# A graph network kernel: four groups of a row norm done by PE and ACT beside the sort, eight more loaded beside it

## The chip, the cores and the metric

One core of one Trainium2 chip. The metric is the device time of one execution in microseconds (us). PE is the matrix engine (TensorE), DVE the vector engine, ACT the scalar engine, POOL is GpSimd, SP only issues transfers.

## The reference, cut to what matters

There are 50,000 nodes with 256 features each and 12,500 edges, sorted by destination.

```python
x = _layernorm(x + gat(x, edges))      # attention over edges, relu(out + bias)
x = _layernorm(x + conv(x, src, dst))  # three max-convolutions with batch norm
def _layernorm(x, axis=-1, eps=1e-05):
    m = jnp.mean(x, axis=axis, keepdims=True)
    v = jnp.var(x, axis=axis, keepdims=True)
    return (x - m) / jnp.sqrt(v + eps)
```

A node that is the destination of no edge gets `relu(bias)` from the attention. So the kernel norms `x + relu(bias)` for all nodes ("the norm of all nodes"), and later overwrites the rows of the nodes that edges lead to.

## The kernel before

**Stages.** (1) The sort: 12,800 keys lie in a tile of 128 x 256 elements; DVE makes a bitonic sort of them (`sort_dve`, line 400 and on). Exchanges inside a partition (lines 426, 427) need only DVE. For k from 8 to 14, exchanges across partitions go by way of PE: DVE flips signs (line 418), PE transposes two blocks of 128 x 128 (line 500, `sort_pe`), DVE exchanges the transposed keys (lines 437 to 441), and the same again back. That is 14 turns, numbered 0 to 13 here; each waits for the one before. (2) `lists_dve` (lines 513 to 535) decodes the keys to lists of indices. (3) The edge stage, 25 tiles of 512 edges: POOL gathers rows of x (line 682, eight gathers a tile), PE turns them (line 696) and multiplies (lines 706, 712), ACT copies between (line 723) and writes h to the large buffer `big` (line 728), DVE copies the scores (line 735), SP stores the destination rows to `x_dst` (line 739) and the scores (line 743). (4) The softmax over edges on DVE (lines 751 to 841). (5) The message stage (from line 873), then three convolutions, the last state, and a dense pass over all rows (lines 1290 to 1343).

**The norm of all nodes** runs beside stages 3 and 4, in 40 groups (0 to 39): 39 of 1280 rows, ten rows to a partition, 1.31 MB each, and a rest of 80 rows. A ring `pre` of four buffers holds them. For group g, ACT's queue issues the load (`pre_load`, line 608). DVE adds relu(bias) to the whole group (line 625), takes statistics of ten rows (line 628) and joins them (line 634) (`pre_stats`). ACT takes the root (line 643, `pre_std`). DVE makes factor and shift with a Newton step in six small instructions (lines 652 to 660, `pre_finish`). ACT norms ten rows (line 668, `pre_norm`) and issues the store (`pre_store`, line 614). The four first loads are issued by ACT at the start, which then has nothing to do until the first edge tile is turned.

**The order of the work** is written by hand, one program for each engine at the end of the function. On DVE, edge tile t is followed by the finish of group t - 1 and the statistics of group t; so 25 groups (`EARLY = NS = 25`) go with the edge tiles, five stand between the steps of the softmax, and ten after it (the tail), before the message stage. On ACT, `pre_turnover(g)` (norm, store, load of the group three further on) stands once in each step of the edge stage. SP issues the setup loads, then waits for the lists. POOL builds constants, gathers for the edge stage, scatters the table of slots (lines 595, 588), and waits for all stores of the norm before its first scatter of message rows (line 964).

PE uses PSUM banks 5 and 6 in the sort and bank 7 for small things; 0 to 4 are unused there. `big` is written first by the edge stage.

Of the kernel before, what the change touches and what calls it, by code (L numbers as in the profile page):

```python
# [50 lines left out]
PRE_RING = 4  # L51
assert 0 < PTAIL <= P
# [5 lines left out]
def gnn(nc, x, src, dst, w, att_src, att_dst, bias, theta_t, phi_t, gammas, betas, out):  # L58
    ctx = ExitStack()
    with ctx:  # L60
# [77 lines left out]
        s_pre_x = [sem(f"pre_x_{b}") for b in range(PRE_RING)]  # L138
        s_pre_sum = sem("pre_sum")
# [107 lines left out]
        pre = part_of(8192, PRE_RING * PR * D).rearrange("p (b r f) -> p b r f", b=PRE_RING, r=PR)  # L247
        stat = sb("stat", [P, 2, PR, 6])
# [56 lines left out]
        def in_steps(stages, count):  # L305

            for s in range(count + max(lag for lag, _ in stages)):
                for lag, f in stages:
                    if 0 <= s - lag < count:
                        f(s - lag)  # L310

# [88 lines left out]
        def sort_dve(v):  # L400
# [30 lines left out]

            def exchange_turned(source, bit):
                nonlocal n, cur
                a = source.rearrange("p (x t b) -> p x t b", t=2, b=1 << bit)
                c = sort_buf[cur].rearrange("p (x t b) -> p x t b", t=2, b=1 << bit)
                o = sort_buf[1 - cur].rearrange("p (x t b) -> p x t b", t=2, b=1 << bit)
                v.tensor_copy(c[:, :, 1, :], a[:, :, 1, :]).then_inc(s_sort, 1)
                n += 1
                done()
                v.tensor_tensor(o[:, :, 0, :], a[:, :, 0, :], c[:, :, 1, :], ALU.min).then_inc(s_sort, 1)  # L440
                v.tensor_tensor(o[:, :, 1, :], a[:, :, 0, :], c[:, :, 1, :], ALU.max).then_inc(s_sort, 1)
                n += 2
                cur = 1 - cur
                done()
# [47 lines left out]
        def sort_pe(pe):  # L492
# [4 lines left out]
            for i, (n, cur) in enumerate(SORT_MARKS):  # L497
                pe.wait_ge(s_sort, n)
# [104 lines left out]
        def pre_load(a, g):  # L603
            rows, p, r = node_rows(g)
            b, u = g % PRE_RING, g // PRE_RING
# [3 lines left out]

        def pre_store(a, g):  # L610
            rows, p, r = node_rows(g)
            b = g % PRE_RING
            a.wait_ge(s_pre_normed, g + 1)
            a.dma_start(x1_dram[rows, :].rearrange("(p r) f -> p r f", r=r), pre[0:p, b, 0:r, :]).then_inc(s_pre_stored[b], 16)

        def rbias_dve(v):
            v.wait_ge(s_bias, 16)
            v.tensor_scalar(rbias_ps, rbias[:, :], 0.0, None, ALU.max).then_inc(s_rbias, 1)
            v.wait_ge(s_rbias, 1)

        def pre_stats(v, g):
            rows, p, r = node_rows(g)
            b, u, e = g % PRE_RING, g // PRE_RING, g % 2
            v.wait_ge(s_pre_x[b], 16 * (u + 1))
            v.tensor_tensor(pre[0:p, b, 0:r, :], pre[0:p, b, 0:r, :], rbias_ps[0:p, :].unsqueeze(1).to_broadcast([p, r, D]), ALU.add).then_inc(s_pre_sum, 1)  # L625
            v.wait_ge(s_pre_sum, g + 1)
            for n in range(r):
                m = v.bn_stats(stat[0:p, e, n, :], pre[0:p, b, n, :])  # L628
            m.then_inc(s_pre_stat, 1)
            v.wait_ge(s_pre_stat, g + 1)  # L630
# [6 lines left out]
        def pre_std(a, g):  # L637
            rows, p, r = node_rows(g)
            e = g % 2
            a.wait_ge(s_pre_mv, g + 1)  # L640
            if g > 1:
                a.wait_ge(s_pre_newton, 4 * (g - 1))
            a.activation(std[0:p, e, 0:r], mv[0:p, e, 0:r, 1], ACT.Sqrt, bias=eps_b[0:p, :]).then_inc(s_pre_std, 1)

        def pre_finish(v, g):
# [7 lines left out]
            v.wait_ge(s_pre_newton, 4 * g + 1)  # L653
            v.scalar_tensor_tensor(d, mv[0:p, e, 0:r, 1], EPS, near, ALU.add, ALU.mult).then_inc(s_pre_newton, 1)
            v.scalar_tensor_tensor(off, mv[0:p, e, 0:r, 0], -1.0, near, ALU.mult, ALU.mult).then_inc(s_pre_newton, 1)
            v.wait_ge(s_pre_newton, 4 * g + 2)
            v.scalar_tensor_tensor(d, d, -0.5, near, ALU.mult, ALU.mult).then_inc(s_pre_newton, 1)
            v.wait_ge(s_pre_newton, 4 * g + 4)
# [3 lines left out]
        def pre_norm(a, g):  # L662
# [3 lines left out]
            for n in range(r):  # L666
                o = pre[0:p, b, n, :]
# [57 lines left out]
        def gat_keep_h(a, t):  # L725
            for j in range(2):
# [139 lines left out]
        def msg_dve(v):  # L866
            v.wait_ge(s_h_kept, 2 * NS)

            def sums(t):
# [9 lines left out]
                else:  # L879
                    v.wait_ge(s_pre_stored[0], 16 * len(range(0, PG + 1, PRE_RING)))  # L880
# [77 lines left out]
        def x1_pool(pl):  # L958
            for b in range(PRE_RING):
                pl.wait_ge(s_pre_stored[b], 16 * len(range(b, PG + 1, PRE_RING)))  # L960
# [42 lines left out]
        def conv_sync(sp, l):  # L1003
            def masks(t):
                if l == 0 and t == 0:
                    for k in range(PRE_RING):
                        sp.wait_ge(s_pre_stored[k], 16 * len(range(k, PG + 1, PRE_RING)))
# [372 lines left out]
        def _(act):  # L1380
            act.wait_ge(s_ids, 32)
            for g in range(PRE_RING):
                pre_load(act, g)
            act.wait_ge(s_const, CONST)
            act.wait_ge(s_params, PARAMS)

            def pre_turnover(g):
                pre_norm(act, g)
                pre_store(act, g)
                if 1 <= g and g - 1 + PRE_RING <= PG:  # L1390
                    pre_load(act, g - 1 + PRE_RING)
            for s in range(NS + 2):
                if s < NS:
                    gat_keep(act, s)
                if 1 <= s <= NS:
                    gat_keep_h(act, s - 1)
                    pre_std(act, s - 1)
                if 2 <= s:
                    pre_turnover(s - 2)
# [100 lines left out]
```

## Time and profile before

| what | us |
|---|---|
| median of 3 runs (2014.74 to 2016.46) | 2015.37 |
| the profiled execution, its own time | 2019.85 |
| its span, from first to last instruction | 2018.1 |
| PE busy | 1183.2 |
| DVE busy | 1293.8 |
| ACT busy | 909.1 |
| POOL busy | 976.3 |
| transfers, 436.12 MB | 216 GB/s mean |

The span is what the rows below are numbered by, from 0. The difference of 1.75 us between the span and the execution's own time lies around it. Busy times overlap: engines run beside each other, and only where one waits for another does a time reach the end. A busy share over the whole span is a mean over stages that have different limits; the rows below are taken stage by stage. In a row of the timeline, the bracket at the end is the idle time of that engine just before, and what ended it. For a float32 product PE shows two records.

### The profile page before, as it was taken

The numbers are of one execution on the slowest core, as the hardware profiler recorded it, in microseconds if no ns is written. First come the engines' busy times: TensorE is split into PE (matmuls) and PEld (weight loads), VectorE is DVE, ScalarE is ACT, GpSimd is POOL, SyncE is SP. The second block draws the span as 40 slices with busy tenths as digits, with TensorE's granted clock in tenths as the row PEclk, the third lists the DMA queues.
The fourth block names the chain that finished last, engine by engine and source line by source line (L and its number), as shares of the span: only waits on it lengthen the run. The fifth ranks groups of instructions, "written<-read, shape, count | busy, mean of one in ns | idle before, by whom it ended". The sixth has DMA issues, their size and how long they took to land. (4 is left out here: it accounts for less than half of the span.)

```text
span 2018.1 us, 16817 instructions
## 1 busy us (share of the span) xinstructions
PE 1183.2 (59%) x3962; PEld 635.5 (31%) x3962; DVE 1293.8 (64%) x3151; ACT 909.1 (45%) x2286; POOL 976.3 (48%) x1033
## 2 busy tenths in 40 slices
PE   1177878730027773699995899969999675000000
PEld 0033333310003331355552455534544564000000
DVE  7746666689879995245553456635666432778887
ACT  0047657664542222244442356634554321556555
POOL 1176565677606777777772764325451577000000
PEclk9999889865555555799997899989999888555555
DMA  3069889987954553588884588747663454898998
GB/s 123 20 187 341 327 315 345 319 252 210 345 195 126 158 165 109 159 255 262 262 258 120 112 175 198 183 126 126 134 140 79 150 182 158 316 356 339 353 349 316
DMA packets 177486, 436.12 MB, mean 216 GB/s; under 512 B 28900, under 2 KB 108906, under 8 KB 157420
## 3 DMA queue, kind: packets, MB, share of 16 engines
q1 hardware_dynamic: 107964, 219.04, 32.0%
q0 software_dynamic: 44800, 100.49, 20.1%
q10 hardware_dynamic: 24624, 115.51, 16.4%
q8 instruction: 33, 0.54, 0.1%
q14 instruction: 65, 0.53, 0.1%
HBM read 257.16 MB, written 182.32 MB: 218 GB/s over the span
## 5 line engine op out<-in xcount | busy, mean ns | idle before, releaser
L1157 DVE TENSOR_TENSOR_SCAN arena<-arena,ps 128x512 f32<-128x512 f32 x150 | 191.3, 1277 | 267.3 <-PE ps L1082 254.3
L1052 POOL DMA_INDIRECT arena<-agg,slot x200 | 189.0, 945 | 206.8 <-PE ps L1072 112.3
L682 POOL DMA_INDIRECT arena<-x,idx x200 | 189.2, 946 | 192.6 <-DVE idx L535 85.5
L1082 PE MATMUL ps<-arena 128*128 128x512 f32 x600 | 276.0, 604 | 0.0
L1092 PE MATMUL ps<-arena 128*128 128x512 f32 x600 | 269.7, 592 | 0.0
L1338 ACT ACTIVATE arena<-arena 128x256 f32<-128x256 f32 x391 | 156.6, 402 | 145.9 <-DVE arena L1307 145.9
L1034 POOL DMA_INDIRECT arena<-x,idx x200 | 189.2, 946 | 62.0 <-issue 59.1
L668 ACT ACTIVATE arena<-arena,shift,inv 128x256 f32<-128x256 f32 x391 | 196.2, 589 | 38.5 <-DVE shift L660 38.5
L927 PE MATMUL ps<-arena,head_of 8*128 8x512 f32 x100 | 93.7, 1088 | 159.1 <-DVE arena L882 119.8
L1161 DVE TENSOR_TENSOR ps<-arena,ps 128x512 f32<-128x512 f32 x150 | 104.1, 696 | 110.4 <-PE ps L1092 110.4
L1072 PE MATMUL ps<-ident,arena 128*128 128x128 f32 x800 | 114.0, 289 | 103.6 <-DMA arena<-agg,slot 50.0
L1128 ACT ACTIVATE arena<-ps,bn_shift,bn_scale 128x512 f32<-128x512 f32 x100 | 72.8, 774 | 215.7 <-PE ps L1072 215.5
L1092 PEld LDWEIGHTS ps<-arena 128*128 128x128 f32 x600 | 114.0, 190 | 143.5 <-issue 142.5
L1307 DVE TENSOR_TENSOR arena<-arena 128x2560 f32<-128x2560 f32 (+1 forms) x40 | 110.6, 2765 | 58.9 <-DMA arena<-x 58.7
L1082 PEld LDWEIGHTS ps<-arena 128*128 128x128 f32 x600 | 110.8, 195 | 111.9 <-issue 101.1
L964 POOL DMA_INDIRECT x<-big,idx x100 | 99.7, 997 | 87.4 <-ACT big L954 56.7
L1276 POOL DMA_INDIRECT x<-arena,idx x100 | 99.4, 994 | 84.8 <-DVE arena L1267 56.0
L1072 PEld LDWEIGHTS ps<-ident,arena 128*128 128x128 f32 x800 | 94.4, 147 | 129.0 <-DMA arena<-agg,slot 52.9
L628 DVE BATCH_NORM_STATS2 stat<-arena 128x6 f32<-128x256 f32 x391 | 131.6, 411 | 1.4
L1120 ACT ACTIVATE arena<-ps 128x512 f32<-128x512 f32 x100 | 55.2, 595 | 170.4 <-PE ps L1072 169.9
L588 POOL DMA_INDIRECT slot<-slot_of,idx x100 | 96.2, 962 | 71.4 <-SPq L1020 35.3
L625 DVE TENSOR_TENSOR arena<-arena,ps 128x2560 f32<-128x2560 f32 (+1 forms) x40 | 110.2, 2755 | 17.6 <-DMA arena<-x 17.6
(183 smaller groups left out, 2155.6 us busy)
## 6 DMA issues: line engine op xcount, KB each, us to landing
arena<-x ACTq DMA_DIRECT2D x39, 1280.0 KB, 10.7
x<-arena ACTq DMA_DIRECT2D x39, 1280.0 KB, 6.5
arena<-x SPq DMA_DIRECT2D x39, 1280.0 KB, 8.2
out<-arena SPq DMA_DIRECT2D x39, 1280.0 KB, 5.4
agg<-arena SPq DMA_DIRECT2D x50, 512.0 KB, 4.7
arena<-not_same SPq DMA_DIRECT2D x75, 256.0 KB, 3.9
arena<-last_of SPq DMA_DIRECT2D x75, 256.0 KB, 5.1
x_dst<-arena SPq DMA_DIRECT2D x25, 512.0 KB, 6.5
```

Source lines behind the costliest of these rows:

```text
L625: v.tensor_tensor(pre[0:p, b, 0:r, :], pre[0:p, b, 0:r, :], rbias_ps[0:p, :].unsqueeze(1).to_broadcast([p, r, D]), ALU.add).then_inc(s_pre ...
L628: m = v.bn_stats(stat[0:p, e, n, :], pre[0:p, b, n, :])
L668: m = a.activation(o, o, ACT.Identity, scale=inv[0:p, b, n:n + 1], bias=shift[0:p, b, n:n + 1])
L682: pl.indirect_dma_start(rows_in[:, par, a, g, :], None, x[:, :], bass.IndirectOffsetOnAxis(ap=idx[:, k, t * G + g:t * G + g + 1], axis=0)) ...
L1034: pl.indirect_dma_start(conv_in[:, b, a, g, :], None, x1_dram[:, :], bass.IndirectOffsetOnAxis(ap=idx[:, k, t * G + g:t * G + g + 1], axis ...
L1052: pl.indirect_dma_start(conv_in[:, b, 1, g, :], None, agg_dram[l - 1][:, :], bass.IndirectOffsetOnAxis(ap=slot[:, t * G + g:t * G + g + 1] ...
L1072: m = pe.transpose(turn_bank[j][:, g * P:(g + 1) * P], conv_in[:, b, a, g, j * P:(j + 1) * P], ident[:, :])
L1082: m = pe.matmul(far_bank[j], thp[:, l, 0, k, j * P:(j + 1) * P], far_t[:, par, k, :], start=(k == 0), stop=(k == 1))
L1092: m = pe.matmul(near_bank[j], thp[:, l, 1, k, j * P:(j + 1) * P], near_t[:, par, k, :], start=(k == 0), stop=(k == 1))
L1157: v.tensor_tensor_scan(runmax[:, par, j, :], mask[:, par, :], far_bank[j], initial, ALU.add, ALU.max).then_inc(s_conv_scan, 1)
L1307: v.tensor_tensor(y, y, c_rows[0:p, :].unsqueeze(1).to_broadcast([p, r, D]), ALU.add).then_inc(s_dense_y, 1)
L1338: m = a.activation(unused[0:p, n, :], y_tile[0:p, b, n, :], ACT.Square, scale=1.0 / ROOT, accum_out=msq[0:p, b, n:n + 1])
```

## The change

Groups 0 to 3 are no longer done by DVE. PE adds the bias: for each of a group's ten rows it multiplies the row tile by the identity and adds the product of a row of ones and relu(bias), into banks 0 to 4 (`rows_pe`). ACT copies the sum back to the ring and sums each row (`rows_sum_act`), makes the negative mean, squares the centred row with a sum (`rows_square_act`), takes the root, and norms as before. DVE keeps the six small instructions (`rows_finish`), three times placed just before it waits for a turn of the sort (turns 1, 5 and 10), the fourth time after the sort. PE does groups 0 and 1 before turn 0, group 2 before turn 2 and group 3 before turn 6. DVE takes relu(bias) before the sort (`row_bias_dve`); after it, a copy goes to PSUM.

Groups 4 to 11 are loaded at the start by SP (`big_load_sync`, after the setup) into the last 80% of `big`, each with its own semaphore, and are normed and stored from there beside edge tiles 0 to 7. ACT waits for the store of such a group before it writes h over it. The ring holds groups 0 to 3 and 12 to 39; its loads follow in that order. The edge stage still has 25 groups beside it, now 4 to 28; five stand in the softmax (29 to 33) and six after it (34 to 39).

```diff
@@ -49,6 +49,8 @@
 PRE_RING = 4
+PRE_SORT = 4
+PRE_BIG = 8
...
@@ -308,6 +320,40 @@
+        def in_big(g):
+            return PRE_SORT <= g < PRE_SORT + PRE_BIG
...
+        RING_USES = PG + 1 - PRE_BIG
...
+        def pre_rows(g):
+            if in_big(g):
+                lo = NS * 2 * SUP - (PRE_SORT + PRE_BIG - g) * PR * D
+                return big[:, lo:lo + PR * D].rearrange("p (r f) -> p r f", r=PR)
+            return pre[:, ring_use(g) % PRE_RING, :, :]
...
@@ -429,6 +475,11 @@
+            def beside_turn():
+                for g, at in enumerate((1, 5, 10)):
+                    if turns == at:
+                        rows_finish(v, g)
...
@@ -457,11 +508,13 @@
             for k in range(8, 15):
                 flip_partition(k - 7)
+                beside_turn()
                 turns += 1
                 v.wait_ge(s_sort_turned, 2 * turns)
...
+                beside_turn()
                 turns += 1
                 v.wait_ge(s_sort_turned, 2 * turns)
...
@@ -495,6 +548,9 @@
             for i, (n, cur) in enumerate(SORT_MARKS):
+                for g, at in enumerate((0, 0, 2, 6)):
+                    if i == at:
+                        rows_pe(pe, g)
                 pe.wait_ge(s_sort, n)
...
@@ -600,34 +656,102 @@
+        def big_load_sync(sp):
+            for k in range(PRE_BIG):
+                rows, p, r = node_rows(PRE_SORT + k)
+                sp.dma_start(pre_rows(PRE_SORT + k), x[rows, :].rearrange("(p r) f -> p r f", r=r)).then_inc(s_big_x[k], 16)
...
+        def row_bias_dve(v):
+            v.wait_ge(s_bias, 16)
+            v.tensor_scalar(rbias[:, :], rbias[:, :], 0.0, None, ALU.max).then_inc(s_rbias, 1)
+
+        def rows_pe(pe, g):
+            if g == 0:
+                pe.wait_ge(s_const, 8)
+                pe.wait_ge(s_rbias, 1)
+            loaded(pe, g)
+            for i in range(PR // 2):
+                if g:
+                    pe.wait_ge(s_row_ready, PR * (g - 1) + 2 * i + 2)
+                for n in range(2 * i, 2 * i + 2):
+                    o = bank[i][:, (n % 2) * D:(n % 2 + 1) * D]
+                    pe.matmul(o, ident[:, :], pre_rows(g)[:, n, :], start=True, stop=False)
+                    m = pe.matmul(o, ones[0:1, :], rbias[0:1, :], start=False, stop=True)
+                m.then_inc(s_row_sum, 1)
+
+        def rows_sum_act(a, g):
+            if g > 1:
+                a.wait_ge(s_row_squares, g - 1)
+            for n in range(PR):
+                a.wait_ge(s_row_sum, PR // 2 * g + n // 2 + 1)
+                a.activation(pre_rows(g)[:, n, :], bank[n // 2][:, (n % 2) * D:(n % 2 + 1) * D], ACT.Identity,
+                             accum_out=row_sum[:, n:n + 1]).then_inc(s_row_ready, 1)
+            a.wait_ge(s_row_ready, PR * (g + 1))
+            a.activation(row_mean[:, g, :], row_sum[:, :], ACT.Copy, scale=-1.0 / D).then_inc(s_row_mean, 1)
+
+        def rows_square_act(a, g):
+            a.wait_ge(s_row_mean, g + 1)
+            for n in range(PR):
+                m = a.activation(row_unused[:, n, :], pre_rows(g)[:, n, :], ACT.Square, bias=row_mean[:, g, n:n + 1],
+                                 accum_out=row_var[:, g, n:n + 1])
...
+            a.activation(std[:, g % 2, :], row_var[:, g, :], ACT.Sqrt, scale=1.0 / D, bias=eps_b[:, :]).then_inc(s_pre_std, 1)
...
@@ -723,6 +846,10 @@
         def gat_keep_h(a, t):
+            for k in range(PRE_BIG):
+                lo = NS * 2 * SUP - (PRE_BIG - k) * PR * D
+                if lo < (t + 1) * 2 * SUP and t * 2 * SUP < lo + PR * D:
+                    a.wait_ge(s_big_stored[k], 16)
...
@@ -1344,11 +1469,12 @@
-        EARLY = NS
+        EARLY = PRE_SORT + NS
...
             setup_sync(sp)
+            big_load_sync(sp)
             lists_sync(sp)
...
             def pre_turnover(g):
                 pre_norm(act, g)
                 pre_store(act, g)
-                if 1 <= g and g - 1 + PRE_RING <= PG:
-                    pre_load(act, g - 1 + PRE_RING)
+                if not in_big(g) and ring_use(g) and ring_use(g) - 1 + PRE_RING < RING_USES:
+                    pre_load(act, ring_use(g) - 1 + PRE_RING)
+            rows_sum_act(act, 0)
+            rows_square_act(act, 0)
+            for g in range(1, PRE_SORT):
+                rows_sum_act(act, g)
+                pre_turnover(g - 1)
+                rows_square_act(act, g)
+            pre_turnover(PRE_SORT - 1)
+            act.wait_ge(s_params, PARAMS)
...
             keys_dve(dve)
+            row_bias_dve(dve)
             sort_dve(dve)
+            rows_finish(dve, PRE_SORT - 1)
             lists_dve(dve)
...
             for t in range(NS):
                 gat_score(dve, t)
                 if t:
-                    pre_finish(dve, t - 1)
-                pre_stats(dve, t)
+                    pre_finish(dve, PRE_SORT + t - 1)
+                pre_stats(dve, PRE_SORT + t)
```

## Rows read from the trace of the kernel before

**Rows 1.** The windows view by stage: window, its length, busy us (instructions) by engine, clock, DMA.

```profile
0.00:27.50 27.50, 0.98 (x8) 0.92 (x8) 22.25 (x75) 0.00 (x0) 7.31 (x33) 1.00 0.62 226
27.50:86.40 58.90, 9.64 (x28) 4.04 (x28) 44.16 (x174) 0.00 (x0) 0.00 (x0) 1.00 0.00 0
...
421.00:500.00 79.00, 3.01 (x13) 1.10 (x12) 75.34 (x190) 39.66 (x79) 62.17 (x56) 0.53 0.81 239
500.00:589.40 89.40, 3.75 (x4) 1.16 (x4) 72.82 (x256) 53.74 (x111) 39.57 (x41) 0.50 0.84 298
```

**Rows 2.** The timeline at the start of the message stage: start, us, engine, line.

```profile
589.38 1.22 DVE L873 TENSOR_TENSOR ps<-ps,big 128x1024 f32<-128x1024 f32 x1
...
614.64 1.02 POOL L964 DMA_INDIRECT x<-big,idx  x1 [56.69 <-ACT big L954]
```

**Rows 3.** The timeline of PE's turns in the sort.

```profile
27.51 0.69 PE L500 MATMUL ps<-ident,arena 128*128 128x128 f32 x2 [22.81 <-DVE arena L418]
...
34.41 0.69 PE L500 MATMUL ps<-ident,arena 128*128 128x128 f32 x2 [4.54 <-DVE arena L418]
...
49.78 0.69 PE L500 MATMUL ps<-ident,arena 128*128 128x128 f32 x2 [4.54 <-DVE arena L418]
```

**Rows 4.** The timeline of DVE where the sort ends and the decoding of the lists begins.

```profile
86.47 0.29 DVE L513 TENSOR_SCALAR arena<-arena 128x256 int32<-128x256 int32 x1
```

**Rows 5.** The first three loads of x, line 608: issue, and issue to landing.

```profile
L608 ACTq DMA_DIRECT2D arena<-x x3: 390/450/1119, 3.6 to 4.5; - x3
...
DMA to landing us min/median/max: 8.5/11.2/13.9
```

**Rows 6.** PE on 128x256 float32 products of line 1250, warm and after a gap.

```profile
1626.80 3.72 PE L1250 MATMUL ps<-center,arena 128*128 128x256 f32 x16 [2.09 <-DVE arena L1259]
...
1692.22 10.10 PE L1250 MATMUL ps<-center,arena 128*128 128x256 f32 x32 [3.28 <-DVE arena L1259]
```

**Rows 7.** Groups and timeline of ACT: a square with sum of one row, ten rows normed.

```profile
L1338 ACT ACTIVATE arena<-arena 128x256 f32<-128x256 f32 x390 | 156.2, 402 | 145.9 <-DVE arena L1307 145.9
...
419.02 5.01 ACT L668 ACTIVATE arena<-arena,shift,inv 128x256 f32<-128x256 f32 x10
```

**Rows 8.** DVE's finish of one group of the norm, first and last instruction.

```profile
458.38 0.21 DVE L652 RECIPROCAL ps<-std 128x10 f32<-128x10 f32 x1
...
459.11 0.16 DVE L660 SCALAR_TENSOR_TENSOR shift<-step,ps 128x10 f32<-128x10 f32 x1
```

**Rows 9.** DVE's copies of the scores, line 735, of tiles 1, 3, 4 and 24.

```profile
132.72 0.68 DVE L735 COPY score<-ps 8x512 f32<-8x512 f32 x1 [1.22 <-PE ps L706]
...
154.80 0.68 DVE L735 COPY score<-ps 8x512 f32<-8x512 f32 x1 [4.74 <-PE ps L706]
163.71 0.68 DVE L735 COPY score<-ps 8x512 f32<-8x512 f32 x1 [0.48 <-PE ps L706]
...
418.69 0.65 DVE L735 COPY score<-ps 8x512 f32<-8x512 f32 x1
```

**Rows 10.** Windows of the edge stage, and the waits that end on transfers.

```profile
93.80:163.70 69.90, 49.36 (x169) 23.60 (x169) 35.87 (x115) 29.32 (x55) 53.12 (x56) 0.93 0.63 197
163.70:421.00 257.30, 204.09 (x632) 90.06 (x632) 168.53 (x568) 171.05 (x345) 159.63 (x169) 0.89 0.92 324
...
POOL arena L682 <- DMA x_dst<-arena: 45.6, 17, 7.8
...
DVE arena L625 <- DMA arena<-x: 17.6, 11, 4.5
```

**Rows 11.** The timeline of DVE, additions of the bias (line 625) in the tail.

```profile
522.53 2.82 DVE L625 TENSOR_TENSOR arena<-arena,ps 128x2560 f32<-128x2560 f32 x1 [3.37 <-DMA arena<-x]
...
556.32 2.81 DVE L625 TENSOR_TENSOR arena<-arena,ps 128x2560 f32<-128x2560 f32 x1
...
564.53 2.81 DVE L625 TENSOR_TENSOR arena<-arena,ps 128x2560 f32<-128x2560 f32 x1
```

More of the change, by code:

```diff
@@ L138, in gnn @@
         s_pre_x = [sem(f"pre_x_{b}") for b in range(PRE_RING)]
+        s_big_x = [sem(f"big_x_{k}") for k in range(PRE_BIG)]
+        s_big_stored = [sem(f"big_stored_{k}") for k in range(PRE_BIG)]
+        s_row_sum = sem("row_sum")
+        s_row_ready = sem("row_ready")
+        s_row_mean = sem("row_mean")
+        s_row_squares = sem("row_squares")
         s_pre_sum = sem("pre_sum")
@@ L310, in in_steps, with ring_use, group_at, loaded @@
                         f(s - lag)
+        def in_big(g):
+            return PRE_SORT <= g < PRE_SORT + PRE_BIG
+        def ring_use(g):
+            return g if g < PRE_SORT else g - PRE_BIG
+        def group_at(use):
+            return use if use < PRE_SORT else use + PRE_BIG
+        RING_USES = PG + 1 - PRE_BIG
[4 more added lines that the diff above has]
+            return pre[:, ring_use(g) % PRE_RING, :, :]
+        def loaded(e, g):
+            if in_big(g):
+                e.wait_ge(s_big_x[g - PRE_SORT], 16)
+            else:
+                e.wait_ge(s_pre_x[ring_use(g) % PRE_RING], 16 * (ring_use(g) // PRE_RING + 1))
+        def all_stored(e):
+            for b in range(PRE_RING):
+                e.wait_ge(s_pre_stored[b], 16 * len(range(b, RING_USES, PRE_RING)))
+            for k in range(PRE_BIG):
+                e.wait_ge(s_big_stored[k], 16)
         def node_rows(g):
@@ L613, in pre_store @@
             a.wait_ge(s_pre_normed, g + 1)
-            a.dma_start(x1_dram[rows, :].rearrange("(p r) f -> p r f", r=r), pre[0:p, b, 0:r, :]).then_inc(s_pre_stored[b], 16)
+            a.dma_start(x1_dram[rows, :].rearrange("(p r) f -> p r f", r=r), pre_rows(g)[0:p, 0:r, :]).then_inc(stored, 16)
+        def row_bias_dve(v):
[14 more added lines that the diff above has]
+                m.then_inc(s_row_sum, 1)
@@ L666, in pre_norm @@
             for n in range(r):
[L667 removed]
+                o = pre_rows(g)[0:p, n, :]
                 m = a.activation(o, o, ACT.Identity, scale=inv[0:p, b, n:n + 1], bias=shift[0:p, b, n:n + 1])
@@ L725, in gat_keep_h @@
         def gat_keep_h(a, t):
+            for k in range(PRE_BIG):
+                lo = NS * 2 * SUP - (PRE_BIG - k) * PR * D
+                if lo < (t + 1) * 2 * SUP and t * 2 * SUP < lo + PR * D:
+                    a.wait_ge(s_big_stored[k], 16)
             for j in range(2):
@@ L879, in sums @@
                 else:
-                    v.wait_ge(s_pre_stored[0], 16 * len(range(0, PG + 1, PRE_RING)))
+                    v.wait_ge(s_pre_stored[0], 16 * len(range(0, RING_USES, PRE_RING)))
                 for j in range(2):
@@ L958, in x1_pool @@
         def x1_pool(pl):
-            for b in range(PRE_RING):
-                pl.wait_ge(s_pre_stored[b], 16 * len(range(b, PG + 1, PRE_RING)))
+            all_stored(pl)
             for t in range(NS):
@@ L1005, in masks @@
                 if l == 0 and t == 0:
-                    for k in range(PRE_RING):
-                        sp.wait_ge(s_pre_stored[k], 16 * len(range(k, PG + 1, PRE_RING)))
+                    all_stored(sp)
                 if l or t > 1:
@@ L1381, in _ @@
             act.wait_ge(s_ids, 32)
-            for g in range(PRE_RING):
-                pre_load(act, g)
+            for use in range(PRE_SORT):
+                pre_load(act, use)
             act.wait_ge(s_const, CONST)
-            act.wait_ge(s_params, PARAMS)
             def pre_turnover(g):
```

62 lines of the change are left out of this document (44 added, 18 removed).

## The prediction

> **What bounds the kernel now.** I read the windows by stage first, then the waits, then the timelines of the stages that the change touches. To 27.5 us DVE sorts inside each partition. From there to 86.4 it sorts across partitions: DVE is busy for 44.16 of 58.90 us, PE for 9.64, ACT not at all, and no byte moves [rows 1]. The sort is a chain between DVE and PE: DVE flips, PE transposes two blocks (0.69 us), DVE goes on. Between turn 1 and turn 2, and between turn 5 and turn 6, PE is idle for 4.54 us [rows 3]. The decoding starts at 86.47 [rows 4]. So three resources lie idle beside a chain that is itself critical: whatever is put on PE there is free only in so far as it fits between two turns.
>
> The edge stage follows, 25 tiles beside 25 groups of the norm. While few node groups move, two tiles take 22.08 us (copy of the scores of tile 1 at 132.72, of tile 3 at 154.80), 11.04 a tile; from tile 4 at 163.71 to tile 24 at 418.69 it is 254.98/20 = 12.75 a tile [rows 9]. In between the transfers went from 197 to 324 GB/s and from 0.63 to 0.92 of the engines; POOL waits 45.6 us in all for the stores of the destination rows, DVE 17.6 us for loads of x [rows 10]. The first pace is a loop over engines (score, statistics, root, norm, copy, product); the rest, 1.71 us a tile, is contention of transfers.
>
> The softmax and the tail follow. DVE is busy for 75.34 of 79 us to 500, and 72.82 of 89.4 us until the message stage starts [rows 1]; it is the bound, with 15 groups of the norm on it. In the tail one group follows the other by 564.53 - 556.32 = 8.21 us, and one stall for a load stands beside the first loads of the message stage [rows 11]. The message stage starts at 589.38, and POOL has by then been idle for long: its first scatter at 614.64 comes after 56.69 us of waiting [rows 2]. All later work starts from there, so what reaches 589.38 reaches the end.
>
> **Part 1, PE ahead of turn 0: +5.9 us.** PE does groups 0 and 1 before it looks at the first turn, each 10 products with the identity and 10 with the row of ones, on 256 columns of float32. A row of the same shape gives 16 records, two for each product, in 3.72 us [rows 6], so 0.2325 us a record; 20 products are 40 records, 9.3 us. After 3.28 us idle 32 records took 10.10 us, 2.7 us more than twice 3.72 [rows 6]: so I price a start from rest at 12.0 us. The first load is issued at 3.6 us and lands 8.5 us later, at 12.1; the second is there by 15.2 (issued near 4, 11.2 us) [rows 5]. Group 0 runs 12.1 to 24.1, group 1 to 33.4. Turn 0 stood at 27.51 [rows 3], so the sort waits 5.9 us. The relu of the bias ahead of the sort vanishes in this wait. SP's eight new loads are issued from 8.7 us on, behind the setup; no wait of SP stands behind them before the lists at 91 us, and their 10.5 MB have 60 us of idle transfer engines, so they cost nothing of their own. If they hold up group 0, the bound is the landing of the second load now, 3.1 us later. The Trainium skill ("DMA: Bandwidth & Descriptors", Queues, rings and completion order) says that each transfer engine serves the queues that have work in turn, packet by packet; by it ACT's first load would share from 8.7 us, and I estimate 1.4 us more for the sum. No row here has two such large queues at once in the setup.
>
> **Part 2, PE between the turns: +4.8 and +7.5 us.** Group 2 stands between turn 1 and turn 2: 9.3 us in a hole of 4.54 us, 4.8 us too many; PE has been busy just before, so I take the warm price. Group 3 stands before turn 6 after some 10 us in which PE only makes short turns with idle stretches as long as 4.54 us; I take the start from rest: 12.0 - 4.54 = 7.5 us. Below, both are warm and group 0 too: 3.2 + 4.8 + 4.8 us. Above, the engine stays at the lower of its two levels, 1.2 GHz, all through: 18.6 us a group, which gives 21.8 + 14.1 + 14.1 us for the three places.
>
> **Part 3, DVE: +1.5 us.** A finish takes 0.89 us (458.38 to 459.27) [rows 8]. Three of the four stand where DVE waits for a turn of 0.69 us anyway, 0.2 us each too many; the fourth, 0.9 us, comes after the sort and before the decoding, on the path. DVE waits in them for ACT's root. ACT has per group ten sums and ten squares, 0.402 us each, and ten norms, 5.01 us [rows 7]: 13 us, 52 for all four groups in a sort that then lasts until 105 us. Root 1 is ready some 10 us before turn 5, root 3 some 9 us before the sort ends; I charge nothing. If that cover were gone, each missing us would stand in the sort. Group 3 is normed and stored beside the decoding and the first gathers; ACT was not needed there before. Its wait for the parameters, now behind this, ends long before. Sort in all: 5.9 + 4.8 + 7.5 + 1.5 = +19.7 us, with bounds 13.7 and 51.4.
>
> **Part 4, the edge stage: -11 us.** It still norms 25 groups, so the loop of 11.04 us stays. But groups 4 to 11 lie in the buffer of h and their turnovers load nothing; groups 12 to 14 are loaded by the turnovers of groups 1 to 3. So for eight tiles 1.31 of some 4.2 MB a tile are gone (gathers 1.05, destination rows 0.52, load and store of a group 1.31 each). At 1.71 us a tile that is 13.7 us if all contention goes. The stores stay, so I take 11. Bounds: 0 (the stores alone are enough), and 20 (the ring also runs ahead afterwards, so that DVE's 17.6 us of waits shrink too). The new waits of ACT for the stores of groups 4 to 11 before it writes h start with tile 5; by then group 4 has been stored for three tiles. Nothing.
>
> **Part 5, the tail: -32.8 us.** Four groups fewer stand behind the softmax: 4 x 8.21 = 32.8 us, all DVE. ACT's norms, four loads and four stores go with them. Next after DVE would be POOL, which has 56.69 us of slack [rows 2]; the stage starts some 24 us earlier, so it holds. Bounds 28 (the stall at the first message loads grows) and 36.
>
> **Sum.** The profiled execution took 2019.85 us (span 2018.1). 2019.85 + 19.7 - 11 - 32.8 = 1995.8. The runs' median 2015.37 lies 4.5 us below the profiled one, so the forecast is **1991.3 us**. What follows the message stage is unchanged.
>
> **Rivals.** (a) *PE at the lower level through the sort.* The place is the 40 records of each group; the price 18.6 instead of 9.3 us; with the sort 51.4 us longer the time is 2015.4 + 51.4 - 43.8 = 2023, slower. It decides from the point where the sort grows by more than 43.8 us. For it: the turns of 0.69 us come from an engine that rests most of the time. Against: groups 0 and 1 are 20 us of unbroken work. 7%. (b) *No relief in the edge stage*: stores and gathers alone keep the transfers late, or the loop is the bound in any case: 2002. For it: two thirds of the traffic remain. 20%. (c) *Both better*: warm everywhere in the sort (+13.7) and 20 us in the edge stage: 1976. 13%. (d) *The tail gives half*: fewer groups, but the first loads of the message and of the weights meet them closer, 16 us: 2008. 5%. (e) *It doesn't do what it says*: a late root of ACT holds DVE in the sort so long that gain and loss are level: about 2015. 2%. My forecast, with 1981 to 2001 as its own range, has 53%.
>
> **Numbers.** A measurement of this kernel can tell about 0.2% (4 us) from no change. The range 1974 to 2008 holds the forecast, (b), nearly all of (c) and a part of (d). Faster 0.91, same 0.02, slower 0.07.
>
> **What would show it.** Turn 0 near 33 us, holes of 9 and 12 us before turns 2 and 6, the decoding near 106 us; PE at both levels before turn 0; the scores' copies 11 to 11.5 us apart in tiles 2 to 10 and 12.7 later; six groups instead of ten between the end of the softmax and the message stage, and its start near 565 us; the conv and dense stages as long as now. Wrong would be: roots of ACT releasing DVE inside the sort, PE at the lower level in groups 1 and 2, POOL or a load as the last wait before the message stage.

## The result, and the profile after

The changed kernel takes 2037.41 us (median of 5, 2033.12 to 2047.74) where the kernel before takes 2015.37: a ratio of 1.0105, 95% interval 1.0084 to 1.0126. It is 22 us slower; the forecast was 24 us faster. The profiled execution is the longest of the five, 2047.74 us (before 2019.85), so its differences come to 27.9 us and not to 22. A run more than 1.5% above the fastest of its kernel is left out of ratios and ranges below; there was one, the profiled one of e1_no_ones.

The windows view of the kernel after (columns as in [rows 1]) has the time to turn 0, the rest of the sort, and two windows around the softmax and the tail.

```profile
0.00:58.40 58.40, 46.94 (x88) 20.88 (x88) 22.18 (x76) 15.54 (x60) 7.33 (x33) 1.00 0.71 286
58.40:154.80 96.40, 54.92 (x109) 24.06 (x108) 47.49 (x199) 40.46 (x140) 0.00 (x0) 1.00 0.18 68
478.00:562.00 84.00, 5.39 (x18) 1.86 (x16) 79.61 (x209) 42.73 (x84) 66.03 (x60) 0.53 0.75 233
562.00:617.00 55.00, 3.75 (x4) 1.16 (x4) 41.08 (x148) 31.58 (x66) 36.84 (x38) 0.50 0.92 285
```

The sort ended at 86.4 us and now ends at 154.8. DVE's work in it is nearly what it was (22.18 + 47.49 us against 22.25 + 44.16 in [rows 1]); PE's grew from 10.6 to 101.9 us. What DVE waited for inside the sort is one line of the waits view (total, times, longest):

```profile
DVE arena L488 <- PE ps L556: 76.1, 11, 31.9
```

It waits for the transposes of the turns (line 556), and those stand behind the row products. No wait of DVE for a root of ACT is in that view. The timeline of PE after (start, us, engine, line; x2 is one float32 product, two records):

```profile
12.44 1.19 PE L694 MATMUL ps<-arena,ident 128*128 128x256 f32 x2 [7.74 <-DMA arena<-x]
13.56 1.22 PE L695 MATMUL ps<-rbias,ones 1*128 1x256 f32 x2
14.71 1.22 PE L694 MATMUL ps<-arena,ident 128*128 128x256 f32 x2
...
57.26 1.22 PE L695 MATMUL ps<-rbias,ones 1*128 1x256 f32 x2
58.41 0.69 PE L556 MATMUL ps<-ident,arena 128*128 128x128 f32 x2
60.08 0.69 PE L556 MATMUL ps<-ident,arena 128*128 128x128 f32 x2 [0.97 <-DVE arena L492]
60.56 1.06 PE L694 MATMUL ps<-arena,ident 128*128 128x256 f32 x2
...
82.25 1.22 PE L695 MATMUL ps<-rbias,ones 1*128 1x256 f32 x2
83.40 0.69 PE L556 MATMUL ps<-ident,arena 128*128 128x128 f32 x2
```

Read the starts, not the durations, which overlap: a product starts 1.15 us after the last, 20 of them are 23.0 us, from the first group to the last. The transposes of the turns between them take 0.69 us each, as before; in e2 below, behind a stream at the upper level, the same ones take 0.38 to 0.44. Turn 0 moved from 27.51 to 58.41, +30.9 us. The turn behind group 2 moved 18.1 us more (23.32 us from turn 1 to turn 2; 5.23 before, 29.18 to 34.41), and the one behind group 3 another 18.1. The lists follow on DVE:

```profile
154.77 0.29 DVE L569 TENSOR_SCALAR arena<-arena 128x256 int32<-128x256 int32 x1
...
192.73 0.68 DVE L862 COPY score<-ps 8x512 f32<-8x512 f32 x1 [26.91 <-PE ps L829]
...
201.84 0.68 DVE L862 COPY score<-ps 8x512 f32<-8x512 f32 x1 [1.49 <-PE ps L829]
...
293.86 0.68 DVE L862 COPY score<-ps 8x512 f32<-8x512 f32 x1 [1.59 <-PE ps L829]
...
479.12 0.65 DVE L862 COPY score<-ps 8x512 f32<-8x512 f32 x1
...
616.96 1.22 DVE L1000 TENSOR_TENSOR ps<-ps,big 128x1024 f32<-128x1024 f32 x1
```

The second to fifth lines are the scores of tiles 0, 1, 10 and 24, the last is the start of the message stage. The ledger against [rows 2, 4, 9]: decoding +68.3 us; from the decoding to score 24, 324.4 us instead of 332.2, -7.9; from there to the message stage, 137.8 instead of 170.7, -32.9; the message stage starts 27.6 us late and the kernel ends 27.9 us late. Nothing of note happened behind it.

### The profile page after: what moved, and what is told of

It is laid out like the page before. It is cut to its first block and busy times, and to the rows that moved or that the text cites. A ratio compares the mean times of both kernels' runs of the same rounds, so it can differ in the third digit from the quotient of the medians.

```text
span 2045.9 us, 17256 instructions
## 1 busy us (share of the span) xinstructions
PE 1265.8 (62%) x4122; PEld 667.8 (33%) x4122; DVE 1266.3 (62%) x3068; ACT 946.1 (46%) x2450; POOL 978.6 (48%) x1033
## 5 line engine op out<-in xcount | busy, mean ns | idle before, releaser
L791 ACT ACTIVATE arena<-arena,shift,inv 128x256 f32<-128x256 f32 (+1 forms) x311 | 156.1, 587 | 71.9 <-DVE shift L731 37.3
L644 POOL DMA_INDIRECT slot<-slot_of,idx x100 | 97.8, 978 | 70.2 <-SPq L1145 33.2
L1090 POOL DMA_INDIRECT x<-big,idx x100 | 99.7, 997 | 50.2 <-issue 30.8
L1375 PE MATMUL ps<-center,arena 128*128 128x256 f32 x400 | 102.2, 417 | 30.4 <-DVE arena L1384 30.4
L651 POOL DMA_INDIRECT slot_of<-slot_of_pos,idx x100 | 106.4, 1064 | 30.5 <-issue 30.5
## 6 DMA issues: line engine op xcount, KB each, us to landing
arena<-x ACTq DMA_DIRECT2D x31, 1280.0 KB, 10.7
```

What stands on the lines that cost most here:

```text
L644: pl.indirect_dma_start(slot[:, c:c + 1], None, slot_dram[:, :], bass.IndirectOffsetOnAxis(ap=idx[:, S_DST, c:c + 1], axis=0)).then_inc(si ...
L791: m = a.activation(o, o, ACT.Identity, scale=inv[0:p, b, n:n + 1], bias=shift[0:p, b, n:n + 1])
```

## The experiments

Where a kernel ran several times, the time is a median and the ratio is to the kernel before on the same chip, with its 95% interval. The kernel before took 2013.47 us beside e1 to e4, 2353.33 beside e5 to e8 (another chip, on which the kernel took some 17% longer but the sort did not; of the profiles made there only the sort is read), 2015.37 beside e9 to e12, 2017.47 beside e13 to e15. "Decoding" is the start of DVE's decoding of the sorted keys: 86.47 before, 154.77 in the changed kernel.

**What in the row work costs so much?** e1_no_ones leaves the product of the ones row out (so groups 0 to 3 are normed without the bias):

```diff
-pe.matmul(o, ident[:, :], pre_rows(g)[:, n, :], start=True, stop=False)
-m = pe.matmul(o, ones[0:1, :], rbias[0:1, :], start=False, stop=True)
+m = pe.matmul(o, ident[:, :], pre_rows(g)[:, n, :], start=True, stop=True)
```

> The changed kernel without the ten products of the row of ones and relu(bias) in each of groups 0 to 3: the bias is left out of these 5,120 rows, the ten products with the identity stay. In the changed kernel each product, of either kind, starts 1.15 us after the one before. Theory K (products with one row of weights keep PE at its lower level, and the switch between one row and 128 rows costs on top): with them gone PE rises to the upper level within the first group, products come 0.47 us apart, groups 0 and 1 end before 27.5 us, the two later holes close, and the sort grows by some 3 us instead of 68: about 1973 us. Theory L (PE is at its lower level in this part of the kernel whatever it does; the sort begins with a rested engine): products 0.83 to 0.95 us apart, 9 us a group, turn 0 near 31, two holes of 4.5 us more each, sort +13: about 1983 us. Theory S (every product costs 1.15 us because the identity's weights are loaded anew each time): still 1.15 us apart, 11.5 us a group, sort +23: about 1992 us.

e2_full_ones keeps both products and gives the second one 128 rows:

```diff
-m = pe.matmul(o, ones[0:1, :], rbias[0:1, :], start=False, stop=True)
+m = pe.matmul(o, ones[:, :], rbias[:, :], start=False, stop=True)
...
-v.tensor_scalar(rbias[:, :], rbias[:, :], 0.0, None, ALU.max)
+v.tensor_scalar(rbias[:, :], rbias[:, :], 0.0, 1.0 / P, ALU.max, ALU.mult)
```

Behind the sort DVE multiplies its copy of the bias by 128 again.

> Same arithmetic, but the bias product has 128 rows: a full matrix of ones times relu(bias)/128 held in all partitions; DVE scales by 1/128 before and by 128 after. Number and columns of the products are those of the changed kernel. Theory K: PE rises to the upper level in the first group; group 0 takes 12 us, group 1 9.3, turn 0 near 34, sort +20 as I had forecast: about 1990 us. Theory L: 0.93 us a product, 18.6 us a group, turn 0 near 50, sort +51: about 2020 us. Theory S: as the changed kernel, 1.15 us a product, 2037 us.

Measured: e1 1963.68 to 1978.97 us in three runs, ratio 0.9781 (0.9742 to 0.9819); its profile is of an execution of 1998.59 us, and of it only the sort is read, with the decoding at 89.24. e2 1982.1 us, 0.9856 (0.9831 to 0.9881), decoding at 100.56, with as many products as the changed kernel. The sorts grew by 2.8 and 14.1 us: theory K's 3 and 20 and not theory L's 13 and 51 or theory S's 23 and 68. The same kernel as e2 was run again on another chip as e15_full_ones:

> e2_full_ones again beside e13_staged on the same chip: 1979 to 1985 on a chip on which the kernel before takes 2014, ratio 0.983 to 0.988.

It took 1992.08 us, 0.9869 (0.984 to 0.9898), decoding at 100.96; the absolute time was above what was expected, the ratio as expected. The start of its PE timeline:

```profile
12.37 1.19 PE L694 MATMUL ps<-arena,ident 128*128 128x256 f32 x2 [7.66 <-DMA arena<-x]
13.35 1.06 PE L695 MATMUL ps<-rbias,ones 128*128 128x256 f32 x2
...
15.91 1.02 PE L694 MATMUL ps<-arena,ident 128*128 128x256 f32 x2
16.76 0.60 PE L695 MATMUL ps<-rbias,ones 128*128 128x256 f32 x2
...
18.06 0.60 PE L694 MATMUL ps<-arena,ident 128*128 128x256 f32 x2
```

Behind the first one, products start 0.85 us apart up to 16.8 us and 0.43 us apart from there, half: the engine went from its lower level (1.2 GHz) to the upper one (2.4 GHz). In the changed kernel none of the 80 products, from 12.4 to 116.9 us, does so. Here the products alternate between the identity and the ones as well, and pay 0.85 us and not 1.15: the change of weights alone is not the price. Making the second product 128 times as tall saves 54 us of sort.

**One half of the change at a time.** e3_sort_only has no early loads into the buffer of h (`PRE_BIG = 0`), e4_big_only has them and no row work in the sort (`PRE_SORT = 0`).

> The first half of the change alone: groups 0 to 3 beside the sort, no group loaded into the buffer of h (PRE_BIG = 0); the ring's loads run on with group 4. If the eight early loads are worth what the traces say (24 intervals of the edge stage 8.4 us shorter), this is slower than the changed kernel by 7 to 13 us: about 2046 us. If the early loads are worth nothing, or delay the first group in the sort, it is 2037 or less. The sort should still be 68 us longer than before in both.

> The second half alone: groups 0 to 7 loaded at the start into the buffer of h, all 40 groups normed by DVE and ACT as before, no work of PE or ACT in the sort (PRE_SORT = 0). The sort should end at 86.5 us as before, tiles 1 to 10 of the edge stage stand 10.2 us apart instead of 11.7, the tail has its ten groups again. Worth 7 to 13 us: about 2006 us. If the relief is given back by tile 24, as the changed kernel's trace shows in part (tiles 10 to 24: 13.2 us against 12.9), it is 2012 or more.

e3: 2052.15 us, 1.0199 (1.0182 to 1.0216). e4: 1995.13 us, 0.9905 (0.9888 to 0.9921). Against 2013.47 that is +38.7 and -18.3, in sum +20.4, where both together gave +22: the parts add. Both show more for the early loads than the 7 to 13 us expected: e4 is 18.3 us faster with them alone, and e3 loses 16.7 us more than the whole change. In e4 the way from the decoding to score 24 fell to 309.0 us (-23.2), in e3 it stayed at 331.0; the early loads alone relieve the edge stage. The 23.2 us are of one profile (see the edge stage again, below).

**Level or change of size?** With 64 rows in place of 128 in e2's two edits (e7_half_ones), and with one identity product of 512 columns for two rows ahead of the two one-row products (e6_pairs):

```diff
+pe.matmul(bank[i][:, 0:2 * D], ident[:, :], pre_rows(g)[:, 2 * i:2 * i + 2, :].rearrange("p r f -> p (r f)"), start=True, stop=False)
 for n in range(2 * i, 2 * i + 2):
     o = bank[i][:, (n % 2) * D:(n % 2 + 1) * D]
-    pe.matmul(o, ident[:, :], pre_rows(g)[:, n, :], start=True, stop=False)
-    m = pe.matmul(o, ones[0:1, :], rbias[0:1, :], start=False, stop=True)
+    m = pe.matmul(o, ones[0:1, :], rbias[0:1, :], start=False, stop=n % 2 == 1)
```

> As e2, with 64 rows of ones and of the bias over 64 in place of 128. If every product that is not of 128 rows keeps PE at its lower level, the sort is as late as in the changed kernel (decoding near 154 us, time 2030 to 2040). If half of the rows is enough (what counts is a share of the array, not the change of size), the records drop from 0.85 to 0.43 us as in e2, decoding near 100 us, time 1978 to 1988. If the change of size costs time of its own, products take more than 0.43 us at the higher level: 0.6 to 0.75, decoding at 110 to 120.

> As the changed kernel, with one identity product of 512 columns for two rows and then the two one-row products of 256 columns, so half as many changes between 128 rows of weights and one. Theory K with a price for the change of weights: a product of 256 columns takes 0.85 and each change 0.30 us more; a bank takes 1.70 + 2 x 0.85 + 2 x 0.30 = 4.0 us instead of 4.6 us, a group 20 us instead of 23.0. Rival: every product has 0.30 us of its own, whatever stood before it: a bank 4.3 us, a group 21.5. In both PE stays at the lower level (no product at 0.43) and the decoding starts at 143 to 149 us, the time is 2018 to 2032.

The timeline of PE in e7_half_ones, then that of e6_pairs:

```profile
15.54 1.22 PE L695 MATMUL ps<-rbias,ones 64*128 64x256 f32 x2
16.69 1.22 PE L694 MATMUL ps<-arena,ident 128*128 128x256 f32 x2
17.84 1.22 PE L695 MATMUL ps<-rbias,ones 64*128 64x256 f32 x2
```

```profile
16.48 2.08 PE L692 MATMUL ps<-arena,ident 128*128 128x512 f32 x2
18.49 2.07 PE L695 MATMUL ps<-rbias,ones 1*128 1x256 f32 x4
20.49 2.08 PE L692 MATMUL ps<-arena,ident 128*128 128x512 f32 x2
```

e7 has the pace of the changed kernel, 1.15 us a product, with the decoding at 154.51 (2377.0 us, ratio 1.010, 1.0034 to 1.0166). A bias product of 64 rows is no better than one of a single row. In e6 a bank takes 4.0 us instead of 4.6, as a price for each change of size gives (1.70 + 2 x 0.85 + 2 x 0.30); a price for each product would have given 4.3. Decoding 143.00 (one execution, 2368.59 us). The changed kernel itself, e8_look, was profiled on this chip too:

> The changed kernel again, unchanged: a second profile of it. If the edge stage gave the relief back for a fixed reason, scores 10 to 24 take 13.2 us each again (12.88 before); if it was this execution, they take 12.1 to 12.5 as in e2, e3 and e4, and the span is 2031 to 2037 instead of 2045.9. The sort is the same: decoding at 154 to 155 us, 1.15 us from one product to the next.

It took 2381.07 us, with the decoding at 154.53; its edge stage says nothing of the faster chips, and e11_look below takes its place.

e9_only_ones then takes the changes of size away and keeps one-row products, by putting one in the place of each identity product (the rows of groups 0 to 3 then hold twice the bias and nothing of x):

```diff
-pe.matmul(o, ident[:, :], pre_rows(g)[:, n, :], start=True, stop=False)
+pe.matmul(o, ones[0:1, :], rbias[0:1, :], start=True, stop=False)
```

> The identity products of the row groups are replaced by a second product of one row of ones: the rows of groups 0 to 3 hold twice the bias and none of x, and PE issues forty one-row products in a row, with no change of weights' size between them. If what keeps PE at the lower level is the one-row product itself, they follow each other at 0.85 us for all forty (turn 0 near 46 us) and no record drops to 0.43. If it is the change between one row and 128, they drop to 0.43 us after the first four to eight, as the products of e2 did, and turn 0 is at 31 to 32 us. In both, the 0.30 us of each change (e6_pairs) is gone: none takes 1.15.

```profile
17.38 1.05 PE L694 MATMUL ps<-rbias,ones 1*128 1x256 f32 x2
18.23 1.06 PE L695 MATMUL ps<-rbias,ones 1*128 1x256 f32 x2
...
44.69 1.06 PE L694 MATMUL ps<-rbias,ones 1*128 1x256 f32 x2
45.54 1.05 PE L695 MATMUL ps<-rbias,ones 1*128 1x256 f32 x2
46.52 0.69 PE L556 MATMUL ps<-ident,arena 128*128 128x128 f32 x2
```

Forty one-row products without a pause, 0.85 us apart behind the first: 34 us of unbroken work and no rise, and the transposes behind them take 0.69 us, those of the lower level. So there are two effects. A stream of one-row products left PE at the lower level where one of 128-row products as dense (e15) did not, and each change between 128 rows and fewer costs 0.30 us on top. Decoding 132.27, 2030.14 us (one execution). Not run was a stream of 64-row products alone: e7 shows that they pay for the change, and not which of the two effects keeps the level down there.

**The products out of the turns' way.** e5_pieces and e10_pieces are one kernel: full-height products in pieces of one or two banks between the turns, all four finishes of DVE in one behind the lists, and so all four norms and stores of ACT behind that:

```diff
-for g, at in enumerate((0, 0, 2, 6)):
-    if i == at:
-        rows_pe(pe, g)
+for g, banks in ROW_PIECES.get(i, ()):
+    rows_pe(pe, g, banks)
...
-    pre_turnover(g - 1)
     rows_square_act(act, g)
-pre_turnover(PRE_SORT - 1)
+for g in range(PRE_SORT):
+    pre_turnover(g)
...
-rows_finish(dve, PRE_SORT - 1)
 lists_dve(dve)
+rows_finish(dve)
```

> The bias product with 128 rows of ones as in e2, and the PE work of the four groups cut into pieces of one or two banks (4 products each) that stand between the turns of the sort: group 0 and two banks of group 1 before turn 0, the other thirteen banks before turns 2, 4, 6 and 7 to 13. The four DVE finishes become one of 6 instructions on 128x40 values, behind the lists. Theory K (one-row products held PE at its lower level; at 128 rows the rest of the +14.1 us of e2's sort is products that stand in a turn's way in blocks): a piece of 4 products takes 3.4 us at 0.85 each or 1.7 us at 0.43, gaps between turns are 4.5 us, so the decoding starts at 87 to 92 us (before 86.47, e2 100.56), the time is 1966 to 1975. Rival: the pieces, each after idle time, all run at 0.85 and those of two banks (6.8 us) stand in the way of turns 8, 12 and 13 by 2 to 3 us each: decoding at 95 to 98, time 1974 to 1982. Rival: ACT cannot empty the banks in time, PE waits for it and the turns with it: decoding beyond 100.

> The kernel of e5_pieces again, beside the kernel before on another chip, if one is given: on the chip of the last call all kernels took 17% longer, in the gathers of the edge and convolution stages. The decoding at 84.7 us again (before 86.47). On a chip on which the kernel before takes 2014 us: e2's 1982 less the 15.9 us by which its sort was later, 1962 to 1970, ratio 0.975 to 0.979.

> As e10_pieces, with no early loads into the buffer of h. If the two parts of the change simply add (22 us of edge stage for the early loads, 34 us behind the softmax for the four groups in the sort), the time is 2014 less 2 (decoding at 84.7) less 34, 1976 to 1984, and e10 is 15 to 22 us faster than this. If they share one relief, the difference is under 8 us.

e5: decoding at 84.66, earlier than before (2333.87 us on the slower chip, 0.9915, 0.9877 to 0.9953). e10: decoding at 83.97, yet 1987.74 us, 0.9864 (0.9845 to 0.9884): 18 us more than the upper end expected, and no better than e2, whose decoding was 16.6 us later. e12, without the early loads, 2001.93 us, 0.9937 (0.992 to 0.9955); it missed by as much, and is 14.2 us above e10 (15 to 22 expected), so the parts still about add. The timeline of ACT in e10 shows where the early decoding went (5.02 is ten rows normed; line 844 evicts the first transposes of the edge stage):

```profile
92.37 5.02 ACT L789 ACTIVATE arena<-arena,shift,inv 128x256 f32<-128x256 f32 x10 [7.16 <-DVE shift L729]
...
110.80 5.02 ACT L789 ACTIVATE arena<-arena,shift,inv 128x256 f32<-128x256 f32 x10 [1.44 <-DMA x<-arena]
115.85 0.33 ACTq L675 DMA_DIRECT2D x<-arena  x1
120.85 0.34 ACTq L664 DMA_DIRECT2D arena<-x  x1
121.29 2.56 ACT L844 ACTIVATE arena<-ps 128x512 f32<-128x512 f32 x5 [5.47 <-DMA x<-arena]
```

PE began to transpose tile 0 at 106.24; its eviction stood behind four norms, four stores and a load that waits until 120.85 for the third store. Score 1 came at 152.04, 68 us behind the decoding; in e2 it was 46.7 us. e13_staged puts three finishes back into the sort, so that ACT's norms run beside it; e14_staged_one_row is e13 with the one-row product:

```diff
-for g, at in enumerate((1, 5, 10)):
+for g, at in enumerate((3, 7, 12)):
...
-rows_finish(dve, PRE_SORT - 1)
 lists_dve(dve)
+rows_finish(dve, PRE_SORT - 1)
```

The pieces of e13 end before turn 12.

> The pieces of e10 with the three finishes back in the sort (now before turns 3, 7 and 12, the fourth behind the lists), so that ACT norms and stores groups 0 to 2 before the sort ends; the pieces end one turn earlier (before turn 12). The theory after e10: its early decoding (83.97) was lost again because all four norms, stores and the load behind the third store stood before ACT's first evictions of the edge stage (first eviction at 121.3 although the gathers had landed at 106; score 1 at 152.04 against 147.24 in e2). Then here the decoding is at 87 to 90 (three finishes of 1.5 us more), score 1 about 47 us behind it, 135 to 137, and the time 1967 to 1975 beside 1988 of e10. Rival: the row work costs about this much wherever it stands, and the time is that of e2 (1979 to 1985).

> As e13_staged with the bias product of one row, as the changed kernel has it: the placement alone. If the shape of the product is the cause, 28 products at 1.15 us before turn 0 put it at 44.5 (27.5 before), pieces of 4.6 us stand in gaps of 4.5 and less, those of 9.2 us delay their turns by 4 to 6 us: decoding at 118 to 128, 30 to 40 us behind e13. If the placement in blocks was the cause, it is within 8 us of e13.

e13: **1973.41 us, 0.978 (0.9757 to 0.9803)**, 44 us below the kernel before and 18.7 below e15 on the same chip. Its waits in the sort, its decoding, scores 1 and 24 and the start of the message stage, in an execution of 1981.23 us:

```profile
DVE arena L488 <- PE ps L559: 7.7, 11, 1.0
```

```profile
85.70 0.29 DVE L572 TENSOR_SCALAR arena<-arena 128x256 int32<-128x256 int32 x1
...
135.93 0.68 DVE L867 COPY score<-ps 8x512 f32<-8x512 f32 x1 [3.00 <-PE ps L834]
...
412.66 0.65 DVE L867 COPY score<-ps 8x512 f32<-8x512 f32 x1
...
551.73 1.22 DVE L1005 TENSOR_TENSOR ps<-ps,big 128x1024 f32<-128x1024 f32 x1
```

76.1 us of waiting became 7.7, score 1 comes 50.2 us behind the decoding (68 in e10), and the message stage starts 37.6 us earlier than before. e14 took 2015.51 us (one execution), decoding at 124.3: 38.6 us behind e13 by the shape of the product alone, and 30.5 us before the changed kernel by the placement alone.

**The edge stage again.** e11_look is the changed kernel in a second profile, on a chip that is as fast as the first.

> The changed kernel unchanged, a second profile of it on a chip as fast as the first one. From the decoding to score 24 the profile of before takes 332.2 us, e4 309.0, e2 310.4, the changed kernel 324.4. If the relief of the early loads is 22 us wherever they are made and the changed kernel's profile was a bad execution, this gives 309 to 313 and a span of 2024 to 2034. If the late start of the edge stage costs it, 322 to 326 again and a span near 2045.

It took 2037.77 us: decoding 154.58, score 24 at

```profile
470.20 0.65 DVE L862 COPY score<-ps 8x512 f32<-8x512 f32 x1
```

so 315.6 us behind the decoding: 16.6 less than before, between the two cases expected. With e4 (309.0), e2 (310.4), e15 (320.8), e14 (321.2), e13 (327.0) and e9 (330.3) the relief beside the same early loads runs from 2 to 23 us; in e10 ACT's norms take more than all of it (336.0).

The waits view shows where the spread lies. Between the decoding and score 24 POOL waits before its gathers, for stores of the destination rows or for PE to turn an earlier tile, 45.6 us before, 25.0 in e4, 26.0 in e2, 31.7 in e11, 39.0 in e15, 40.0 in e13, 41.6 in the changed kernel, 52.6 in e9. What is left of the way is 278 to 287 us in each. In the changed kernel, e9, e13 and e15, 25 to 38 us of the waits are three or four waits for PE, of up to 10.6 us; e11 and e2, the same kernels as the changed one and e15, have none. What brings these on was not settled.

## Why the prediction was wrong, by its own steps

**The step that failed is the price of a product in parts 1 and 2.** They took 0.2325 us a record, and 12.0 us for a group from rest, from a row of products with 128 rows [rows 6], and used it for all 20 products of a group, though half of them have one row. Measured: 23.0 us a group, above even the 18.6 given for the lower level. Turn 0 came at 58.41 and not at 33.4 (+30.9 for +5.9), and the two holes cost 18.1 us each for 4.8 and 7.5. With the finishes the sort grew by 68.3 us; forecast 19.7, upper bound 51.4. (The bounds add up to 14.3 and 51.5 with the 1.5 us of part 3, a slip of no weight.) "PE at the lower level in groups 1 and 2", which the prediction names as a sign of being wrong, is what the timeline shows. Everything else is small beside that: 1995.8 + 48.6 (sort) + 3.1 (edge stage) = 2047.5, and the profiled execution took 2047.74.

For products that are all 128 rows tall the step was right and a little high: in e2_full_ones group 0 takes 10.7 us and group 1 8.6. The turns of PE in e2_full_ones:

```profile
31.55 0.38 PE L556 MATMUL ps<-ident,arena 128*128 128x128 f32 x2
32.91 0.44 PE L556 MATMUL ps<-ident,arena 128*128 128x128 f32 x2 [0.98 <-DVE arena L492]
41.82 0.38 PE L556 MATMUL ps<-ident,arena 128*128 128x128 f32 x2
...
51.41 0.69 PE L556 MATMUL ps<-ident,arena 128*128 128x128 f32 x2 [2.04 <-DVE arena L473]
63.15 0.38 PE L556 MATMUL ps<-ident,arena 128*128 128x128 f32 x2
```

Turn 0 is 4.0 us late (5.9 forecast), turn 1 to turn 2 takes 8.91 us instead of 5.23 (+3.7, forecast 4.8), turn 5 to turn 6 11.74 (+6.5, forecast 7.5), the decoding is 14.1 us late (19.7).

**Rival (a) named the place and the first half of the mechanism**, PE at its lower level all through the sort, with 7%. What was held against it, "20 us of unbroken work", is no argument for products of one row, as e9 shows: 34 us of them, unbroken, stay at 0.85. The Trainium skill ("TensorE: Matmul & The Clock Gate", What's actually happening) says that the clock follows how busy the engine has been; if busy means busy in time, e9 would by that have risen as e2 did. Its trace disagrees, and the measurement decides: here a stream that is as dense but one row tall did not raise it. The rival's price lacked the second half, 0.30 us for each change between 128 rows and fewer. The Trainium skill ("TensorEngine Tiling (Array Packing)", Key Properties) says that a change of the tiling mode drains the engine. The traces would fit that, 1.15 us with one-row products between (as much with 64 rows, e7) against 0.85 without the change (e9), if a product of fewer rows counts as another mode; no run here shows that, or the drain itself.

**Part 1, the loads.** The first product began at 12.44 us, 12.1 forecast. The 1.4 us more that was estimated from the Trainium skill ("DMA: Bandwidth & Descriptors", Queues, rings and completion order) did not come; 0.3 did, and without the early loads the first product began no more than 0.5 us sooner (11.94 in e3, 12.16 in e12). PE never waited for a second load.

**Part 3** held: no wait for a root, and the fourth finish took 1.05 us, from 153.72 to the decoding. ACT's squares came 0.49 us apart and not 0.402, at no cost here.

**Part 4** was -11 and came out as -7.9, with -16.6 in e11_look. That it came near is in part luck. The pace of tiles 1 to 10 was better than forecast, 92.02/9 = 10.22 us (11 to 11.5 forecast, 11.74 before), below even the 11.04 that the prediction took for the loop over the engines; that alone is 13.6 us. The pace of tiles 10 to 24 was worse, 185.26/14 = 13.23 (12.7 forecast, 12.88 before), and gave 4.9 us back. The first holds in every profile with the early loads on the faster chips (10.18 to 10.28; 11.74, 11.87 and 12.25 without, before, in e12 and in e3); the second is what varies (12.14 in e4 to 13.66 in e9). e3 and e4 show that it belongs to the early loads, and e4's 23.2 lies above the bound of 20.

**Part 5** held: -32.8 forecast, -32.9 measured (-29 to -35 in the other kernels with the four groups in the sort), six groups instead of ten behind the softmax, and POOL's first scatter still came after 19.4 us of waiting, so POOL was not the bound. What was not foreseen is that ACT's share of the row work can take the path behind the sort, as in e10; in the changed kernel it does not, because the long sort hides it.

## What to carry to other kernels

Adding a bias row with a one-row product of ones is small in arithmetic, not in time: price a product by a row of its own shape, and in a stream of 128-row products give the bias 128 rows of ones and a 128th of its value. Work put on an idle engine beside a critical chain should be cut to the chain's gaps, and must not stand ahead of anything that the chain needs; after it is off one engine's path, look at the next engine's queue (here ACT's norms before the first evictions).

## What the runs showed that was not expected

A stream of one-row float32 products of 256 columns, 40 of them back to back, kept 0.85 us a product to its end; products of 128 rows went from 0.85 to 0.43 in every run with such products alone, in e13 in the fifth, in e5 in the seventh. The level also falls again: in e13, behind two turns with 1.3 and 1.0 us idle before them, products are 0.85 us apart from 30.0 to 32.6 us and 0.43 from 33.2 on. Between a product of 128 rows and one of 1 or 64 rows stand 0.30 us more.

The granted clock in the windows view reads 1.00 in the changed kernel's sort, and in that of the kernel before [rows 1], although the transposes and products there have the durations of the lower level (0.69 and 1.15 us; 0.44 for the same transposes in e2 after a dense stretch). In e13, where the level changes, the same view (the clock is the third number from the end) has

```profile
27.50:85.70 58.20, 33.95 (x132) 25.55 (x132) 46.84 (x193) 43.87 (x156) 0.00 (x0) 0.81 0.54 217
```

In these traces, where the level has not yet changed once, the durations tell it and the column doesn't.

One chip took 2353 us for the kernel for which three others took 2013 to 2017, with the same sort; the difference lay in the later stages (of the 343 us between e8_look and e11_look, one kernel, 165 lie between the decoding and score 24).
